# Attention units in tile order 0, 3, 1, 2; query products by pairs of tiles in two PSUM banks; the further 64 query latents held twice

## The chip, the cores and the metric

One core of one Trainium2 chip runs the whole kernel as one program. The metric is device time in microseconds (us); smaller is better. TensorE is called PE here, VectorE DVE, ScalarE ACT, GpSimd POOL and SyncE SP, as in the profile. A busy PE is not the same as a PE at its peak: a matmul's record has a drain behind the time for which it streams, and the next one starts beside that drain.

## The reference

Two layers on 4 sequences of 512 tokens with 256 features: latent attention with 16 heads, a mixture of 64 experts with 6 per token and a shared expert, a state-space layer, and a gated feed-forward layer with scales. All four are added to the residual. The change is in the attention, cut here to what matters:

```python
q = rmsnorm(x @ w_qa, q_norm_w) @ w_qb          # 192 latents -> 16 heads x (128 + 64)
q_nope, q_rope = q[..., :128], q[..., 128:]
kv = x @ w_kva                                  # 64 latents + 64 rotated key features
kv = rmsnorm(kv_c, kv_norm_w) @ w_kvb
q_rope, k_rope = rotate(q_rope), rotate(k_rope)
scores = einsum('blhd,bmhd->bhlm', q, k) / sqrt(192)
attn = softmax(where(causal_mask, scores, -1e30))
out = einsum('bhlm,bmhd->blhd', attn, v).reshape(B, L, 2048) @ w_o
```

## The kernel before, in words

The key and value weights are folded into the query and output weights beforehand (`prep_queries` L377, `prep_values` L392). So a head has 128 query features: 64 that meet the key's latents and 64 rotated ones. For each of the 4 sequences b, `project` (L452) makes the latents, and `latents` (L794) scales them into `cq1` (128 latents x 512 tokens) and `cq2` (the further 64 latents; rows 64 to 127 of `cq2` and `wqe2` are zeros that POOL writes at L979 and L980).

A **group** g is 4 heads of a sequence; a sequence has 4 groups, hg 0 to 3. A group has 16 **units**, u = 0 to 15: unit u is one head of one tile of 128 queries, tile i = u // 4, head u % 4. A causal tile i has (i+1) x 128 keys, so units are 128, 256, 384 and 512 wide, four of each, in this order. PE, ACT and DVE each walk the group in 16 **slots**, an order written out by hand:

- PE, `slot` L561: `scores` of unit `at` (L529, and a masking matmul in bf16, L530), a piece of the next group's query work, `transposes` of unit `at` - 3 (L538), then `values` (L555) at some slots. Each float32 matmul has two records in the trace.
- DVE, `slot` L886: `maximum` of unit `at` (L861), the reciprocal of the sum of unit `at` - 1 (L866), `evacuate` of unit `at` - 3 (L881, L884), `normalize` of unit `at` - 1 (L872), then perhaps a piece of the routing of the sequence before (`route_slot` L823; `weigh`, L1130, at slots 10, 12 and 14 of hg 2 and 3).
- ACT, `slot` L724: `exps` of unit `at` (L708), then copies of query products (`q_copy` L687, copy at L689), of their transposes (`qt_copy` L691, copy at L693) or of values (`take_values` L712, copy at L720).

Four PSUM banks hold scores, two transposes, one values (bank 6, `VALUE`), one the query products and their transposes (bank 7, `QUERY`). For the next group, `q_product` (L484) of tile i runs at slots 1, 3, 5, 7: `cq1` by 512 columns of weights (L488) and `cq2` by the same number (L489), both over 128 rows of the array. Each tile's product is copied by ACT, rotated by `rope` (L963: L972 to L976, POOL for these) and transposed (`q_transpose` L492, L494) at slots 9, 11, 13, 15. `values` runs three times per group, with tiles (0, 1), (2) and (3), at slots 12, 16 and 20; the last two fall into slots 0 and 4 of the group that follows. It writes two halves of the output's partitions (0 to 63 and 64 to 127), each from 64 columns of weights.

Between sequences PE runs `project`, `mean_squares` (L468, L469, L473), the `output` of the sequence (L617) and `first_queries` (L498): the four products of the next sequence's first group, in banks 7 and 6 in turn, and then their transposes. There POOL rotates tiles 0 and 2, DVE tiles 1 and 3 (`first_ropes` L808). In sequence b >= 1, PE also has in hg 0 the normalised tokens' transposes and the router's logits (`route_slot` L595, L1027), and in hg 1 the counts (L1035, L1036). POOL sends the tokens of the sequence before in hg 3's turns and after them (`att_pool` L978, sends at L1196).

What sets the order: every engine takes its instructions in program order, so a wait at one holds all behind it. A few of the waits:

```python
need(pe, A["exp"], NU * g + u - 3)              # scores(u): exp of unit u-4 done
pe.wait_ge(A["norm"], NU * g + u + 1)           # transposes(u)
pe.wait_ge(A["qs"], TB * (g + 1) + i)           # product i: copy of product i-1 done
pe.wait_ge(A["qte"], TB * (g + 1) + i)          # transpose i: copy of transpose i-1 done
act.wait_ge(A["max"], NU * g + u + 1)           # exp(u)
```

## Time and profile before

| | |
|---|---|
| median of 3 runs | 1339.31 us (1338.85 to 1340.66) |
| the profiled execution | 1338.7 us |
| its span | 1336.9 us |
| PE / DVE / ACT / POOL busy, share of the span | 92% / 61% / 34% / 28% |
| attention, from the first scores to the end of the last group | 58.8 us to about 620 us |
| mean granted TensorE clock | 0.967 of full speed |

The profiled execution's own time, 1338.7 us, is its span and 1.8 us around it. Rows below give the start of an instruction in us from the span's start and its duration. "<-" names what ended a wait.

### The profile page before, as it was taken

The page shows a single profiled execution, that of the slowest core. Times are in us where ns is not written, and L with a number is a line of the kernel's source. Part 1 is how long each engine was busy: PE and PEld are TensorE (multiplying, and loading weights), DVE is VectorE, ACT ScalarE, POOL GpSimd, SP SyncE. Part 2 cuts the span into 40 slices and gives each one's busy share as a digit, 9 for nine tenths or more (in the row PEclk, how much of TensorE's full clock was granted, in tenths as well). Part 3 has the DMA queues.
Part 4 walks back from the last instruction along what each step waited for, and adds up shares of the span by engine and source line. Part 5 has one row for each costly group of instructions (what it writes and reads, how often), then busy time and mean ns, then how long its engine had stood idle before and what let it go on. Part 6 is the DMA issues. An engine that isn't in the chain of part 4 may idle for free.

```text
span 1336.9 us, 19470 instructions
## 1 busy us (share of the span) xinstructions
PE 1231.2 (92%) x6004; PEld 760.4 (57%) x6004; DVE 813.2 (61%) x2238; ACT 454.2 (34%) x1041; POOL 378.8 (28%) x464
## 2 busy tenths in 40 slices
PE   6999999999999899998989999997578899899988
PEld 3566566555655556556556777775235446465454
DVE  6367767787578966785533333334576776676431
ACT  2455525453445425452201111110232533424311
POOL 1243013362425412362250000115364271510200
PEclk9799999999999999999999999998679899999999
DMA  9999999999900100011348888983111011100000
GB/s 317 413 420 420 420 421 419 420 419 417 420 35 28 68 1 1 1 52 44 101 129 256 259 266 273 285 260 118 48 55 48 24 52 36 37 12 17 0 16 16
DMA packets 89422, 235.48 MB, mean 176 GB/s; under 512 B 12769, under 2 KB 23681, under 8 KB 89089
## 3 DMA queue, kind: packets, MB, share of 16 engines
q1 hardware_dynamic: 70912, 192.54, 38.9%
q0 software_dynamic: 9216, 25.18, 5.9%
q10 hardware_dynamic: 9216, 16.78, 3.3%
q8 instruction: 42, 0.69, 0.2%
q14 instruction: 36, 0.29, 0.1%
HBM read 66.70 MB, written 167.77 MB: 175 GB/s over the span
## 4 chain that ended last, share of the span: by engine, by line
PE 69%; DVE 23%; issue 4%; POOL 2%; ACT 1%; DMA 1%; SPq 1%; ACTq 0%; POOLq 0%; DVEq 0%
PE bank L1329 5%; PE bank L529 5%; PE bank L617 4%; PE bank L488 4%; PE bank L1309 4%; PE bank L489 4%; PE bank L555 4%; DVE negmax L861 4%; PE bank L1582 3%; DVE r L872 3%; PE bank L1571 3%; PE bank L1565 3%; PE bank L538 3%; PE bank L1335 3%; PE bank L1294 2%
## 5 line engine op out<-in xcount | busy, mean ns | idle before, releaser
L708 ACT ACTIVATE r<-bank,negmax 128x128 f32<-128x128 f32 (+3 forms) x256 | 135.2, 528 | 174.3 <-DVE negmax L861 173.8
L529 PE MATMUL bank<-r 128*128 128x512 f32 (+3 forms) x512 | 184.3, 443 | 0.0
L861 DVE TENSOR_REDUCE negmax<-bank 128x1 f32<-128x128 f32 (+3 forms) x256 | 124.5, 487 | 44.6 <-PE bank L530 41.6
L972 POOL TENSOR_TENSOR r<-r,tables 128x256 f32<-128x256 f32 x56 | 42.0, 749 | 330.5 <-ACT r L689 330.3
L538 PE MATMUL bank<-tables,r 128*128 128x128 f32 x640 | 115.0, 278 | 12.2 <-DVE r L872 11.6
L1196 POOL DMA_INDIRECT sent<-r,slots x96 | 93.9, 978 | 99.8 <-DVE slots L1117 40.1
L1411 DVE COPY r<-bank 128x512 f32<-128x512 f32 x64 | 41.2, 686 | 120.5 <-PE bank L1335 76.2
L538 PEld LDWEIGHTS bank<-tables,r 128*128 128x128 f32 x640 | 72.7, 141 | 65.9 <-DVE r L872 31.4
L872 DVE TENSOR_SCALAR r<-r,rrow 128x128 f32<-128x128 f32 (+3 forms) x256 | 104.5, 408 | 0.3
L529 PEld LDWEIGHTS bank<-r 128*128 128x128 f32 x512 | 77.8, 191 | 23.6 <-issue 18.3
L1210 POOL DMA_INDIRECT r<-sent,slots x20 | 21.7, 1085 | 219.1 <-DVEq L1409 212.8
L1367 ACT ACTIVATE r<-bank 128x512 f32<-128x512 f32 x32 | 19.1, 597 | 184.8 <-PE bank L1309 184.8
L1525 POOL TENSOR_TENSOR r<-tables,r 128x1024 f32<-128x1024 f32 x16 | 33.8, 2113 | 142.2 <-DVE r L1946 119.6
L488 PE MATMUL bank<-r 128*128 128x512 f32 x128 | 70.0, 629 | 3.6 <-DVE x L816 1.6
L881 DVE COPY late<-bank 128x256 f32<-128x256 f32 (+1 forms) x128 | 60.7, 474 | 15.8 <-PE bank L538 15.7
L489 PE MATMUL bank<-r 128*128 128x512 f32 x128 | 66.3, 599 | 0.0
L1329 PE MATMUL bank<-r 128*128 128x256 f32 x256 | 63.8, 392 | 0.0
L1309 PE MATMUL bank<-r 128*128 128x256 f32 x256 | 61.7, 384 | 0.0
L617 PE MATMUL bank<-spent,r 128*128 128x256 f32 x256 | 57.9, 383 | 0.5 <-ACT r L720 0.5
L1571 PE MATMUL bank<-xnT,late 128*128 128x512 f32 (+1 forms) x96 | 48.6, 632 | 8.8 <-DVE spent L1599 8.8
L530 PE MATMUL bank<-futureb,identb 128*128 128x128 bf16 x256 | 56.1, 219 | 0.0
L1329 PEld LDWEIGHTS bank<-r 128*128 128x128 f32 x256 | 46.0, 189 | 17.2 <-issue 6.2
(266 smaller groups left out, 2390.5 us busy)
## 6 DMA issues: line engine op xcount, KB each, us to landing
sent<-gath SPq DMA_DIRECT2D x8, 16384.0 KB, 94.3
r<-waT_dram SPq DMA_DIRECT2D x64, 304.0 KB, 3.4
r<-sent SPq DMA_DIRECT2D x64, 256.0 KB, 3.4
sent<-r ACTq DMA_DIRECT2D x64, 256.0 KB, 4.1
w2buf<-wcT_dram SPq DMA_DIRECT2D x64, 48.0 KB, 3.5
r<-w_o_dram SPq DMA_DIRECT2D x1, 2048.0 KB, 11.0
sent<-gath SPq DMA_DIRECT2D x2, 1024.0 KB, 57.0
out_dram<-x SPq DMA_DIRECT2D x4, 512.0 KB, 2.9
```

The costliest lines, as they stand in the source:

```text
L488: nc.tensor.matmul(bank[at][:], cq1[:, i * P:(i + 1) * P], w1, start=True, stop=False)
L489: nc.tensor.matmul(bank[at][:], cq2[:, i * P:(i + 1) * P], w2, start=False, stop=True)\
L529: nc.tensor.matmul(at[:, 0:n], QT[g % 2][:, h, i * P:(i + 1) * P], KT[:, 0:n], start=True, stop=False)
L538: last = nc.tensor.transpose(bank[TRANS[u % 2]][:, j * P:(j + 1) * P], prob[:, u % 4, j * P:(j + 1) * P], ident)
L617: last = nc.tensor.matmul(bank[4 + i % 2][:, 0:DIM], OT[:, c, i * P:(i + 1) * P], wvo[:, c, :], start=(c == 0), stop=(c == HEADS // 2 - 1))
L708: nc.scalar.activation(prob[:, u % 4, 0:(i + 1) * P], bank[SCORE[u % 4]][:, 0:(i + 1) * P], ACT.Exp, bias=negmax[:, u:u + 1], scale=1.0, a ...
L861: nc.vector.tensor_reduce(negmax[:, u:u + 1], bank[SCORE[u % 4]][:, 0:(i + 1) * P], axis=AX.X, op=ALU.max, negate=True).then_inc(A["max"], 1)
L872: nc.vector.tensor_scalar(p, p, rrow[:, u:u + 1], None, ALU.mult).then_inc(A["norm"], 1)
L1196: nc.gpsimd.indirect_dma_start(sent[:, :], bass.IndirectOffsetOnAxis(ap=slots[:, t, k:k + 1], axis=0), xn1[:, n // TOPK, :], None).then_in ...
L1309: last = nc.tensor.matmul(bank[2][:, t * ROWS:(t + 1) * ROWS], wb[:, 2 * q + t, k * EI:k * EI + EA], tokens(q, t, k), start=(k == 0), stop ...
L1329: nc.tensor.matmul(to[t][:, half * DIM:(half + 1) * DIM], hid_a[:, q % 2, c:c + P], wb[:, 2 * q + t, KC * EI:KC * EI + DIM], start=(half = ...
L1571: last = nc.tensor.matmul(bank[up][0:w, :], fuT[:, k, lo:lo + w], xnT[:, k, row_tokens(f)], start=(k == 0), stop=(k == KC - 1))
```

## The change

- **Order of units.** `unit(u)` gives tile and head: units 0 to 7 alternate tile 0 and tile 3 over the 4 heads, units 8 to 15 tile 1 and tile 2. All of a tile's query work follows `ORDER` = (0, 3, 1, 2).
- **Values** run twice per group, tiles (0, 3) at slot 12 and (1, 2) at slot 20 (slot 4 of the next group).
- **Query products of two tiles at once.** `q_products(g, m)` makes tiles ORDER[2m] and ORDER[2m+1]. Bank 7 takes heads 0 and 1 of both, bank 6 heads 2 and 3 of both. Part 0: four matmuls of 256 columns with `cq1` over 128 rows. Part 1: four of 256 columns with `cq2` over 64 rows, rows 0 to 63 for bank 7 and 64 to 127 for bank 6. `cq2` holds the 64 latents twice, in both halves, and `wqe2` holds half of the heads in each half; the zeros and POOL's two memsets go. In a group hg 0 part 0 is at slots 1 and 3, otherwise at 6 and 8; part 1 is in the slot behind. ACT copies both banks in part 1's slot.
- **Turns** (transposes of the next group's queries): slots 9, 11, 13, 15 in hg 0; otherwise 11, 13, 14, 15.
- **Routing** of the sequence before is placed anew: the transposes at slots 6 and 8 and the logits at 10 (before 3, 6, 9); DVE's top and select one slot later; counts at slot 2 of hg 1 (before 7), and DVE's part behind them at slots 3 to 10 (before 8 to 15). `weigh` stays. POOL makes eight sends ahead of hg 3's turns rather than two behind each.
- **First queries of a sequence**: both pairs whole, one behind the other; the second waits for the copies of the first. POOL rotates the third tile once the second pair is copied.
- **Preparation**: the fourth bank goes, ACT makes 3 copies rather than 4, and DVE writes `cq2` twice (L800).

```diff
-        PRODUCT_AT = {1: 0, 3: 1, 5: 2, 7: 3}
-        TURN_AT = {9: 0, 11: 1, 13: 2, 15: 3}
-        VALUES_AT = {12: 0, 16: 1, 20: 2}
-        VALUE_TILES = ((0, 1), (2,), (3,))
+        Q_BANKS = (QUERY, VALUE)
+        PRODUCTS_AT = ({6: 0, 8: 1}, {1: 0, 3: 1})
+        TURN_AT = ({11: 0, 13: 1, 14: 2, 15: 3}, {9: 0, 11: 1, 13: 2, 15: 3})
+        VALUES_AT = {12: 0, 20: 1}
+        VALUE_TILES = ((0, 3), (1, 2))
+        ORDER = (0, 3, 1, 2)
+        def unit(u):
+            return VALUE_TILES[u // (2 * HG)][u % 2], u // 2 % HG
...
-            def q_product(g, i, at):
+            def q_products(g, m, parts=(0, 1)):
                 hg = g % GROUPS
...
+                two = 2 * QE
+                w2 = wqe2[:, 2 * hg:2 * hg + 2, :].rearrange("p h c -> p (h c)")
+                for t in range(2 if 0 in parts else 0):
+                    for half in range(2):
+                        w1 = wqe1[:, hg * HG + 2 * half:hg * HG + 2 * half + 2, :].rearrange("p h c -> p (h c)")
+                        nc.tensor.matmul(bank[Q_BANKS[half]][:, t * two:(t + 1) * two], cq1[:, q_tile(ORDER[2 * m + t])], w1,
+                                         start=(t == 0), stop=False)
+                for t in range(2 if 1 in parts else 0):
+                    for half in range(2):
+                        r = slice(QL2 * half, QL2 * (half + 1))
+                        last = nc.tensor.matmul(bank[Q_BANKS[half]][:, t * two:(t + 1) * two], cq2[r, q_tile(ORDER[2 * m + t])],
+                                                w2[r, :], start=False, stop=(t == 1))
+                        if t:
+                            last.then_inc(A["q"], 1)
...
             def first_queries(b):
...
+                pe.wait_ge(A["cq"], 3 * b + 3)
+                q_products(g, 0)
+                pe.wait_ge(A["qs"], TB * g + 2)
+                q_products(g, 1)
...
-                    if i == 0:
+                    if m == 0:
                         pe.wait_ge(A["qte"], TB * g + TB)
+                        need(pe, A["ote"], 2 * g)
...
                     else:
-                        pe.wait_ge(A["qs"], TB * (g + 1) + i)
-                    q_product(g + 1, i, QUERY)
+                        pe.wait_ge(A["qs"], TB * (g + 1) + 2)
+                    q_products(g + 1, m, (0,))
+                if not final and with_next and at - 1 in PRODUCTS_AT[first]:
+                    q_products(g + 1, PRODUCTS_AT[first][at - 1], (1,))
...
+            def q_copies(g, m):
+                two = 2 * QE
+                for half in range(2):
+                    act.wait_ge(A["q"], TB * g + 2 * m + half + 1)
+                    nc.scalar.copy(qs[:, 2 * m:2 * m + 2, half * two:(half + 1) * two],
+                                   bank[Q_BANKS[half]][:].rearrange("p (t c) -> p t c", t=2)).then_inc(A["qs"], 1)
...
+                    for half in range(2):
+                        nc.vector.scalar_tensor_tensor(out=cq2[QL2 * half:QL2 * (half + 1), :], in0=bank[1][0:QL2, :],
+                                                       scalar=qn2[:], in1=rq[0:QL2, :], op0=ALU.mult, op1=ALU.mult)\
+                            .then_inc(A["cq"], 1)
...
-                pool.wait_ge(A["qs"], TB * g + i + 1)
+                pool.wait_ge(A["qs"], TB * g + 2 * (i // 2) + 2)
```

## Rows read from the trace of the kernel before

**Rows 1.** The page's part on busy time: us, share, instructions.

```profile
PE 1231.2 (92%) x6004; PEld 760.4 (57%) x6004; DVE 813.2 (61%) x2238; ACT 454.2 (34%) x1041; POOL 378.8 (28%) x464
```

**Rows 2.** Windows, one group each: length, busy PE, PEld, DVE, ACT, POOL, clock, DMA.

```profile
82.83:111.02 28.19, 28.19 (x163) 17.22 (x160) 19.79 (x66) 15.54 (x44) 9.49 (x16) 1.00 1.02 420
...
226.18:257.01 30.83, 29.63 (x166) 17.96 (x164) 23.22 (x79) 15.40 (x46) 9.36 (x16) 1.00 1.02 420
257.01:287.54 30.53, 28.81 (x162) 17.21 (x160) 25.21 (x89) 15.51 (x46) 17.65 (x24) 1.00 1.02 419
287.54:308.16 20.62, 19.95 (x124) 11.77 (x121) 18.95 (x83) 10.08 (x34) 12.68 (x13) 1.00 1.02 418
139.23:158.99 19.76, 19.49 (x123) 11.73 (x121) 17.37 (x63) 10.88 (x35) 0.00 (x0) 1.00 1.03 420
```

**Rows 3.** Groups by line, 0 to 600 us, the query products.

```profile
L488 PE MATMUL bank<-r 128*128 128x512 f32 x128 | 70.0, 629 | 3.6 <-DVE x L816 1.6 <-issue 1.5
...
L489 PE MATMUL bank<-r 128*128 128x512 f32 x128 | 66.3, 599 | 0.0
```

**Rows 4.** Timeline of PE around `values` (L555) and `mean_squares` (L473).

```profile
75.89 0.50 PE L538 MATMUL bank<-tables,r 128*128 128x128 f32 x3
...
76.32 1.51 PE L555 MATMUL bank<-late,r 128*64 128x256 f32 x12
...
77.77 1.13 PE L529 MATMUL bank<-r 128*128 128x512 f32 x2
...
172.37 3.72 PE L617 MATMUL bank<-spent,r 128*128 128x256 f32 x16
...
176.02 1.12 PE L473 MATMUL bank<-r,ones 64*128 64x512 f32 x2
...
177.07 7.17 PE L617 MATMUL bank<-spent,r 128*128 128x256 f32 x32
```

**Rows 5.** Timeline of the weight loads of one 128-column unit.

```profile
88.07 0.30 PEld L529 LDWEIGHTS bank<-r 128*128 128x128 f32 x2
```

**Rows 6.** Timeline of one 512-wide unit on its way from scores to normalised.

```profile
80.42 0.22 PE L530 MATMUL bank<-futureb,identb 128*128 128x128 bf16 x1
...
80.67 0.69 DVE L861 TENSOR_REDUCE negmax<-bank 128x1 f32<-128x512 f32 x1
...
81.35 0.54 DVE L881 COPY late<-bank 128x384 f32<-128x384 f32 x1
81.40 0.69 ACT L708 ACTIVATE r<-bank,negmax 128x512 f32<-128x512 f32 x1 [0.43 <-DVE negmax L861]
...
81.81 0.48 DVE L872 TENSOR_SCALAR r<-r,rrow 128x512 f32<-128x512 f32 x1
...
82.20 0.68 DVE L861 TENSOR_REDUCE negmax<-bank 128x1 f32<-128x512 f32 x1
...
82.92 0.69 ACT L708 ACTIVATE r<-bank,negmax 128x512 f32<-128x512 f32 x1 [0.74 <-DVE negmax L861]
...
83.60 0.58 ACT L693 COPY r<-bank 128x512 f32<-128x512 f32 x1
```

**Rows 7.** Timeline of the first queries of sequence 1.

```profile
188.80 1.12 PE L488 MATMUL bank<-r 128*128 128x512 f32 x2 [0.52 <-DVE x L816]
...
194.92 0.72 POOL L972 TENSOR_TENSOR r<-r,tables 128x256 f32<-128x256 f32 x1 [1.08 <-ACT r L689]
...
195.97 0.59 ACT L689 COPY r<-bank 128x512 f32<-128x512 f32 x1 [1.13 <-PE bank L489]
...
196.55 0.72 POOL L976 TENSOR_TENSOR r<-r 128x256 f32<-128x256 f32 x1
...
198.97 0.39 PE L529 MATMUL bank<-r 128*128 128x128 f32 x2
```

**Rows 8.** Timeline of DVE around one `weigh` in hg 3 of sequence 1.

```profile
302.60 0.27 DVE L1133 SCALAR_TENSOR_TENSOR scratch<-r,scratch 128x64 f32<-128x64 f32 x1
...
303.54 0.56 DVE L861 TENSOR_REDUCE negmax<-bank 128x1 f32<-128x384 f32 x1
```

More of the change, by code:

```diff
@@ L385, in prep_queries @@
                                  start=True, stop=True)
-                last = nc.tensor.matmul(bank[6 + h // 8][0:QL2, c:c + KVL], wqbT[:, h, P:QL], wkvT[:, 0, h, :],
+                r, c = QL2 * (h // 2 % 2), (h // 4 * 2 + h % 2) * KVL
+                last = nc.tensor.matmul(bank[6][r:r + QL2, c:c + KVL], wqbT[:, h, P:QL], wkvT[:, 0, h, :],
                                         start=True, stop=True)
@@ L394, in prep_values @@
             loaded(pe, "w_o")
[L395 removed]
+            pe.wait_ge(prep_out, 3)
             pe.wait_ge(A["kr"], 1)
@@ L406, in prep_queries_out @@
             act.wait_ge(prep_w, 1)
-            for m in range(2):
-                for dst, b, n in ((wqe1, 4, P), (wqe2[0:QL2], 6, QL2)):
-                    nc.scalar.copy(dst[:, 8 * m:8 * m + 8, 0:KVL],
-                                   bank[b + m][0:n, :].rearrange("p (h c) -> p h c", h=8)).then_inc(prep_out, 1)
+            for dst, at in ((wqe1[:, 0:8], 4), (wqe1[:, 8:16], 5), (wqe2, 6)):
+                nc.scalar.copy(dst[:, :, 0:KVL], bank[at][:].rearrange("p (h c) -> p h c", h=8)).then_inc(prep_out, 1)
         def prep_values_out(act):
@@ L522, in scores @@
             def scores(g, u):
-                i, h = u // HG, u % HG
+                i, h = unit(u)
                 n = (i + 1) * P
@@ L533, in transposes @@
             def transposes(g, u):
-                i = u // HG
+                i, _ = unit(u)
                 pe.wait_ge(A["norm"], NU * g + u + 1)
@@ L543, in values @@
                 tiles = VALUE_TILES[n]
[L544 to L545 removed]
+                pe.wait_ge(A["pte"], NU * g + 2 * HG * (n + 1))
+                need(pe, A["ote"], 2 * g + n)
                 if n == 0 and g % GROUPS == 0:
                     need(pe, R["lgs"], g // GROUPS)
[L548 to L551 removed]
+                for m, i in enumerate(tiles):
+                    c = 2 * P * m
                     for j in range(i + 1):
@@ L704, in exps @@
             def exps(g, u):
-                i = u // HG
+                i, _ = unit(u)
                 act.wait_ge(A["max"], NU * g + u + 1)
@@ L717, in take_values @@
                 hg = g % GROUPS
-                for i in tiles:
-                    c = 2 * P * (i - tiles[0])
+                for m, i in enumerate(tiles):
+                    c = 2 * P * m
                     last = nc.scalar.copy(OT[:, 2 * hg:2 * hg + 2, i * P:(i + 1) * P],
@@ L858, in maximum @@
             def maximum(g, u):
-                i = u // HG
+                i, _ = unit(u)
                 dve.wait_ge(A["s"], NU * g + u + 1)
@@ L868, in normalize @@
             def normalize(g, u):
-                i = u // HG
+                i, _ = unit(u)
                 p = prob[:, u % 4, 0:(i + 1) * P]
@@ L993, in att_pool @@
                 for hg in range(1, GROUPS):
+                    if b and hg == GROUPS - 1:
+                        send_ready(pool, b - 1)
+                        for n_sent in range(2 * TB):
+                            send(b - 1, n_sent)
                     for i in range(TB):
                         turn(GROUPS * b + hg, i)
-                        if b and hg == GROUPS - 1:
-                            if i == 0:
-                                send_ready(pool, b - 1)
-                            send(b - 1, 2 * i)
-                            send(b - 1, 2 * i + 1)
                 if b:
```

143 lines of the change are left out of this document (62 added, 81 removed).

## The prediction

> **What bounds the kernel now.** I read the busy times first: PE is busy for 92% of the span, DVE for 61% [rows 1]. An average over stages says little, so the windows of single groups came next [rows 2]. Of sequence 0's group 1 (28.19 us) PE is busy for all of it, DVE for 19.79 us, 1.24 us per slot. The last group of sequence 0, which has no query work for a next one, takes 19.76 us: DVE needs 17.37, so the two run close. In sequences 1 to 3 groups hg 1 and 2 take 30.83 and 30.53 us; the reader should see that PE's busy share falls there and DVE's rises. So attention is bound by PE where products are made, with DVE near behind elsewhere.
>
> **What PE saves.** A record of 512 columns streams for 0.43 us: two matmuls are four such records, and the groups by line give 0.55 and 0.52 us of union per record [rows 3], drains and half clock included, while the timeline gives 0.86 us for the two records of L473 less the joints below. So a product of one tile costs 1.72 us, of which L489 0.86.
>
> The price of changing the array's shape can be read off a timeline [rows 4]. L538's three records start at 75.89 and stream 0.32; `values` starts at 76.32, 0.11 late. Its 12 records of 256 columns (0.216 us each alone) take 1.45 us until the next start, where six steps of two at once make 1.30; L529 then loses 0.11 more (1.13 against 1.02). Together about 0.45 us per `values`, and the halves do run at once. For 64 rows of the array: L617's 16 records stream 3.46 from 172.37, and L473 starts 0.19 behind that; it takes 1.05 for 0.86. Counting the slow first record behind the joint, I take 0.40 us per stretch of 64 rows.
>
> - *Part 1.* Two tiles' L489 cost 1.72. After: four matmuls of 256 columns, eight records; two at once make four steps, 0.86, plus 0.40. Saved 0.45 per pair, in 24 pairs inside groups: 10.8. No row shows two halves of the array's rows at work at once, only halves of the columns [rows 4]. Bounds: fully together (saves 0.45) and one after the other (costs 0.40). Each half needs a 128-column weight load per record; loads are 0.11 us apart [rows 5], so two fit a step of 0.216. I take fully together, by the nearest row, `values`.
> - The Trainium skill ("TensorE: Matmul & The Clock Gate", Part 3, on packing small matmuls) states 3.07 times for four row tiles, not 4; by that share two tiles would give about 1.5 times, an estimate, part 1 would cost 1.15 + 0.40, the pair would save 0.17 rather than 0.45, and the whole would come out at 1355. The trace shows no such loss for column halves [rows 4], and the sum stays with them.
> - *Values* lose one joint of three per group: 16 x 0.45 = 7.2. The same ten steps of work stay.
> - *Half as many starts of a product behind the bf16 matmul*: 24 x 0.06 = 1.4, an estimate from the 0.05 us by which such a first record runs over.
> - *Preparation*: one ACT copy of 0.5 us less before the first product: 0.5. The second `cq2` write on DVE (0.73 us, as the first) lies beside PE's prep matmuls in sequence 0 and beside L617 in the others; without that cover it would cost 4 x 0.73. The two memsets of POOL are off the path. POOL's eight sends ahead of hg 3's turns take about 8 x 1.27 = 10 us and begin some 4 us before hg 2 does; the first copy there comes about 14 us in, so they are hidden.
>
> Sum of savings: 19.9 us.
>
> **What it adds in waits.** PE's queue is in order, and the pieces now sit so that the next one is due before its copy is made. The chain of a unit [rows 6]: masking matmul at 80.42, maximum at 80.67, exp at 81.40; exp to the next ACT work 0.68 (82.92 to 83.60). So ACT is free 0.25 + 0.73 + 0.68 = 1.66 us after the masking matmul's start of a 512-wide unit, 1.42 of a 384-wide one (maximum and exp some 0.12 shorter each).
>
> 1. *Second pair, slot 8 (hg 1, 2).* From slot 7's masking matmul: part 1 ends at 1.29; ACT, behind its exp, copies two banks from 1.66 to 2.81 (0.55 and 0.59). PE does part 1, one transpose and a 256-wide score, and is ready at 1.92. Wait 0.94, 8 groups: 7.5. In hg 0 part 1 stands beside a 128-wide unit: copies end at 2.5, PE is ready at 2.24: 4 x 0.3 = 1.2.
> 2. *Turn at slot 14.* The one at 13 and this one share bank 7. The copy of the former stands behind exp 13: 1.42 + 0.58 + 0.05 = 2.05; PE is ready after 0.06 + 0.44 + 0.22 + 0.49 = 1.21. Wait 0.84, 8 groups: 6.7. The turn at 15 has a full slot between and waits for nothing.
> 3. *Slots 0 to 4.* Before, light units of DVE and PE came together. Now each two slots hold a long and a short unit: DVE needs some 1.2 us in every slot, but PE only 3.4 in slots 0 to 3 together. DVE's slot: maximum to evacuation to normalise to next maximum 80.67, 81.35, 81.81, 82.20 [rows 6], 1.53 with a 512-wide maximum and normalise; with the other kinds of neighbours 1.06 to 1.22. Following both queues from slot 15, unit 1 is normalised 5.1 us in, while PE stands at its transpose at 4.4: a wait of 0.8 counting the step from one engine to the next. 12 groups: 9.6. Against it: the counts fill it in 3 groups (-2.4), before had such waits of 0.5 in four groups hg 3 and six groups of sequences 1 to 3 (-5.0); `weigh` at slot 14, 0.94 us [rows 8], makes it longer in 3 groups (+2.9). Net 5.1.
> 4. *Slots 5 to 12 without products.* In hg 3 PE's work from slot 5 to the transposes of unit 9 is 6.0 us, DVE's chain is 8.2 (1.08 to 1.40 a slot, and 1.65 us from a 512-wide maximum to its reciprocal): wait 2.25, against some 0.85 before: 4 x 1.4 = 5.6. In hg 0 turns fill some: 1.35 in sequence 0; in the others the router's parts fill it but wait for ACT's copies at slots 7 and 9 and for the logits' copy at 12: 1.5 each. Together 11.4.
> 5. *First queries of sequences 1 to 3* [rows 7]. Before, four products in two banks ran without a wait, the last copy ended at 196.56 (7.76 after 188.80), scores came at 198.97 (10.17). After: a pair takes 3.0; copies to 4.3; the second pair to 7.3; copies to 8.6. Only then does POOL rotate the third tile: 2.35 us (194.92 to 197.27), so until 11.05, and two transposes of 0.45 follow. Scores come at 12.1. 3 x 1.9 = 5.7. In sequence 0 the value preparation (L401, 3.7 us) stands between and covers it.
>
> Sum of added waits: 8.7 + 6.7 + 5.1 + 11.4 + 5.7 = 37.6 us.
>
> **What it takes away in waits.** Sequences 1 to 3 before: hg 1 took 30.83 where sequence 0's took 28.19 [rows 2], of the 2.64 the counts are 0.87 and slot 0's wait 0.5 (counted above); hg 2 was 2.34 longer, 0.5 of it at slot 0. The rest, 3 x (1.3 + 1.8) = 9.3, are turns that wait while DVE routes ahead of a maximum. The routing of hg 1 now lies at slots 3 to 10, beside PE's long slots. I take 8.2 as given back; the bounds are 0 and 9.3.
>
> The sum: -19.9 + 37.6 - 8.2 = +9.5 us on the profiled execution's 1338.7, so 1348.2. The median of the runs is 0.6 above that execution, within their spread; I say 1348. The expert loop and all behind attention stay as they are.
>
> The Trainium skill has a rule that speaks against the change ("TensorEngine Tiling (Array Packing)", PSUM Bottleneck): when tiling makes TensorE faster, the copies out of PSUM may become the limit. The trace bears this out in a way of its own [rows 6], since a copy stands behind the exp; the sum would be the same without it.
>
> **Rivals.**
> - *Faster, the waits of DVE don't form.* Items 3 and 4 rest on my walk through two queues. For it: PE waits at slots 8 and 14 give DVE slack, DVE is busy 19.79 of 28.19 [rows 2], and POOL and ACT are idle half the time. Against: DVE's lead isn't stored, it can't run before the scores are there. Without items 3 and 4 the sum is 9.5 - 16.5 = -7.0: 1332. If the slot 8 and 14 waits are also half as long, -14: 1325. It decides at the point where DVE's slot costs less than PE's over slots 0 to 3, some 0.85 us.
> - *Row halves one after the other.* Part 1 then costs 1.72 + 0.40 rather than 1.26: 24 x 0.86 = 20.6 and 5 in first queries: 1374. For it: no row shows them together; against it: `values` shows halves of columns together, and loads at 0.11.
> - *The routing's waits stay* (nothing given back): 1356.
>
> **How the numbers follow.** Forecast (waits outweigh the saving): 0.54, of it 0.08 within 0.2%; DVE's waits small: 0.34, of it 0.05 within 0.2%; halves in turn: 0.12. 0.2%, about 2.7 us, is what a measurement of this kernel can tell from no change. So faster 0.30, same 0.13, slower 0.57. The range reaches down to 1326, which leaves the fastest outcomes of the first rival out, and up to 1364, which leaves out the halves in turn. The forecast's own range is 1341 to 1358.
>
> **What would show it.** Right: group 1 of sequence 0 at about 29.3 us rather than 28.19; PE waits of nearly 1 us for ACT's product copies at slot 8 and for the copy of a turn at slot 14; L538 waiting for DVE's L872 in slots 4 to 10; part 1's eight records in about 0.86 us; first queries of a sequence 12 us long. Wrong: sequence 0's group 1 under 28 us; or part 1's records at 0.216 us intervals one by one; or, if hg 1 and 2 of sequences 1 to 3 stay over 30.5, the relief.

## The result

The changed kernel takes 1381.41 us (median of 4 runs, 1378.28 to 1388.24), the kernel before 1339.92 beside it on the same chip. The ratio is 1.0317, with a 95% interval of 1.0278 to 1.0357: slower, and outside the range of 1326 to 1364. The direction was right, the size was not. The profiled executions have spans of 1379.8 and 1336.9 us, so the traces differ by 42.9 us. The profiled execution of the changed kernel took 1382.0 us, inside the spread of its four runs.

The profile's page after (busy times, the clock's slices, three of the groups by line):

```profile
PE 1222.5 (89%) x6260; PEld 786.3 (57%) x6260; DVE 828.0 (60%) x2242; ACT 445.2 (32%) x1040; POOL 380.8 (28%) x462
...
PEclk9899999999999999999999999999589999999999
...
L554 PE MATMUL bank<-tables,r 128*128 128x128 f32 x640 | 117.8, 282 | 25.7 <-DVE r L896 25.1
...
L501 PE MATMUL bank<-r 128*128 128x256 f32 x256 | 65.0, 398 | 20.3 <-ACT r L710 13.6
...
L513 PE MATMUL bank<-tables,r 128*128 128x128 f32 x256 | 38.1, 276 | 21.0 <-ACT r L715 10.2
```

PE's share is down from 92% [rows 1] to 89%. L554, the transposes of the softmax weights (L538 before), is the same 640 records, but PE stands 25.7 us in front of them. Before it was this, from the page of the kernel before:

```profile
L538 PE MATMUL bank<-tables,r 128*128 128x128 f32 x640 | 115.0, 278 | 12.2 <-DVE r L872 11.6
```

In front of the part 0 products (L501) and of the turns (L513) it now stands 20 and 21 us, mostly for ACT's copies L710 and L715.

The windows of single groups after, which answer to [rows 2] (hg 1 of sequence 0; hg 3 of sequence 0; hg 0, 1 and 2 of sequence 1):

```profile
84.17:114.02 29.85, 27.58 (x178) 18.60 (x176) 20.21 (x67) 14.55 (x44) 9.63 (x16) 1.00 1.02 420
...
143.72:165.11 21.39, 19.53 (x126) 11.96 (x124) 17.74 (x61) 10.83 (x35) 0.00 (x0) 1.00 1.02 418
...
207.49:237.30 29.81, 27.18 (x174) 19.43 (x172) 19.20 (x67) 15.92 (x44) 9.21 (x16) 1.00 1.02 420
237.30:271.26 33.96, 29.02 (x183) 19.34 (x181) 26.39 (x89) 15.06 (x45) 12.93 (x19) 1.00 1.02 420
271.26:302.74 31.48, 27.73 (x179) 18.59 (x176) 23.82 (x87) 14.46 (x44) 15.01 (x22) 1.00 1.02 420
```

The first two rows are near what was forecast: 29.85 us (29.3 forecast, 28.19 before) and 21.39 (21.2 by item 4 alone, 19.76 before). The other three aren't. Hg 1 of sequence 1 takes 33.96 us where it took 30.83, and hg 0 29.81 where before it took this:

```profile
199.19:226.18 26.99, 26.53 (x146) 16.76 (x144) 18.64 (x71) 15.70 (x42) 9.40 (x16) 1.00 1.02 420
```

Adding the groups by kind, from the masking matmul of one group's first unit to that of the next, and the forecast's terms in the same way (all in us):

| stretch | before | after | measured | forecast |
|---|---|---|---|---|
| 4 groups hg 0 | 104.2 | 114.8 | +10.6 | +1.2 |
| 4 groups hg 1 | 121.1 | 131.7 | +10.6 | hg 1 and 2 |
| 4 groups hg 2 | 119.1 | 124.0 | +4.9 | together -4.7 |
| 4 groups hg 3, to their last unit | 81.6 | 88.4 | +6.8 | +7.9 |
| 3 passages between sequences | 125.7 | 131.3 | +5.6 | +5.7 |
| ahead of the first unit, behind the last | 785.1 | 789.5 | +4.4 | -0.5 |
| sum | 1336.8 | 1379.7 | +42.9 | +9.6 |

(The forecast's terms are rounded one by one here; its sum was 9.5.) One thing shifts between these rows, and the column of the forecast leaves it out. With tiles (0, 3) first and 384- and 256-wide units last, a group does more of its own values and transposes before it ends and hands less to what follows. Counting PE's records in the two traces by their columns (0.43 us for 512), the new order moves 5.2 us of work into the four groups hg 0 and 0.9 into hg 3, out of the passages (4.5) and the last stretch (1.5); no work is added by it. Against a forecast with this shift in it, hg 0 is 4.2 us over, hg 1 and 2 together 20.2, the passages 4.4 and the last stretch 6.4, while hg 3 is 2.0 under. So the passages only seem to come out as forecast: of the 33 us that are missing, most lies in hg 1 and 2 of sequences 1 to 3, which route the sequence before, and some 11 in the passages and behind attention.

**How the pieces look in the trace.** Part 1 with 64 rows of the array, in slot 9 of that first group:

```profile
101.84 0.22 PE L546 MATMUL bank<-futureb,identb 128*128 128x128 bf16 x1
...
101.99 1.14 PE L506 MATMUL bank<-r 64*128 64x256 f32 x8
...
103.06 0.33 PE L554 MATMUL bank<-tables,r 128*128 128x128 f32 x1
```

Eight records of 256 columns (0.216 us each alone) take 1.07 us until the next start (L554 at 103.06). One by one they begin in pairs 0.007 us apart, at 101.992 and 101.999, then at 102.312, 102.528 and 102.744: the two halves of the array's rows work at once. The first pair starts 0.15 behind the masking matmul and holds 0.32 instead of 0.216; part 1 costs about 1.2 us in all, and 1.26 was forecast. The rival "row halves one after the other" falls here, and so does the theory below that they cost more than they save.

The turn at slot 14 of the same group:

```profile
110.35 0.58 ACT L730 ACTIVATE r<-bank,negmax 128x384 f32<-128x384 f32 x1 [0.84 <-DVE negmax L885]
...
110.92 0.58 ACT L715 COPY r<-bank 128x512 f32<-128x512 f32 x1
...
111.64 0.63 PE L513 MATMUL bank<-tables,r 128*128 128x128 f32 x4 [0.77 <-ACT r L715]
```

The turn waits for the copy of the former, which stands behind an exp. From masking matmul to masking matmul the slot takes 2.43 us, of which its work makes 1.47: a wait of 0.96, forecast 0.84. At slot 8 it is 1.02 by the same reckoning, forecast 0.94. (The profile's idle time, 0.77 and 0.82 us, is shorter, because a record's drain covers the start of a wait.)

The routing in sequence 1's hg 1, slots 6 to 8, is where the forecast fails:

```profile
248.30 0.41 DVE L1117 TENSOR_TENSOR r<-scratch,bank 128x256 f32<-128x256 f32 x1
...
248.86 1.97 PE L501 MATMUL bank<-r 128*128 128x256 f32 x8 [1.33 <-DVE r L1117]
...
252.62 0.43 DVE L1123 TENSOR_TENSOR r<-r,scratch 128x256 f32<-128x256 f32 x1
...
253.08 0.69 DVE L885 TENSOR_REDUCE negmax<-bank 128x1 f32<-128x512 f32 x1
...
254.48 1.06 ACT L710 COPY r<-bank 128x512 f32<-128x512 f32 x2
...
255.60 1.99 PE L501 MATMUL bank<-r 128*128 128x256 f32 x8 [1.61 <-ACT r L710]
```

Two waits, both on DVE's account. The pair of slot 6 overwrites a bank that DVE's ranks (L1117) still read, so it stands 1.33 us. Then DVE routes (L1123 at the last) ahead of the maximum of slot 7; maximum, exp and the two copies behind it all slide, and the pair of slot 8 stands 1.61 us. Slots 6 and 8 take 4.64 and 4.74 us here, 3.14 and 3.95 in sequence 0.

In hg 0 of sequence 1 the same happens with the router's copies, which ACT makes behind its exps. PE waits 1.23 us at slot 8 (below) and 0.83 at slot 10:

```profile
221.35 0.69 ACT L730 ACTIVATE r<-bank,negmax 128x512 f32<-128x512 f32 x1 [1.44 <-DVE negmax L885]
222.03 0.57 ACT L361 COPY xnT<-bank 128x512 f32<-128x512 f32 x1
222.66 0.66 PE L355 MATMUL bank<-tables,r 128*128 128x128 f32 x4 [1.23 <-ACT xnT L361]
```

### The profile page after: what moved, and what is told of

The parts are those of the page before. It is cut to its first block, busy times and chain, and to the rows that moved or that the text cites. A ratio compares the mean times of both kernels' runs of the same rounds, so it can differ in the third digit from the quotient of the medians.

```text
span 1379.8 us, 19972 instructions
## 1 busy us (share of the span) xinstructions
PE 1222.5 (89%) x6260; PEld 786.3 (57%) x6260; DVE 828.0 (60%) x2242; ACT 445.2 (32%) x1040; POOL 380.8 (28%) x462
## 4 chain that ended last, share of the span: by engine, by line
PE 62%; DVE 24%; issue 5%; ACT 4%; POOL 2%; DMA 1%; SPq 1%; ACTq 0%; POOLq 0%; DVEq 0%
PE bank L501 5%; PE bank L569 5%; PE bank L1351 4%; PE bank L1331 4%; DVE negmax L885 4%; PE bank L1604 3%; PE bank L1593 3%; PE bank L545 3%; DVE r L896 3%; PE bank L1587 3%; PE bank L636 3%; PE bank L1357 2%; PE bank L1316 2%; PE bank L1338 2%; PE bank L554 2%
## 5 line engine op out<-in xcount | busy, mean ns | idle before, releaser
L545 PE MATMUL bank<-r 128*128 128x256 f32 (+3 forms) x512 | 183.6, 441 | 0.0
L554 PE MATMUL bank<-tables,r 128*128 128x128 f32 x640 | 117.8, 282 | 25.7 <-DVE r L896 25.1
L554 PEld LDWEIGHTS bank<-tables,r 128*128 128x128 f32 x640 | 72.5, 142 | 72.8 <-DVE r L896 49.6
L896 DVE TENSOR_SCALAR r<-r,rrow 128x128 f32<-128x128 f32 (+3 forms) x256 | 101.2, 395 | 0.3
L501 PE MATMUL bank<-r 128*128 128x256 f32 x256 | 65.0, 398 | 20.3 <-ACT r L710 13.6
L501 PEld LDWEIGHTS bank<-r 128*128 128x128 f32 x256 | 47.1, 194 | 35.5 <-ACT r L710 20.2
L905 DVE COPY w2buf<-bank 128x512 f32<-128x512 f32 x64 | 43.6, 681 | 37.2 <-PE bank L554 37.2
L1351 PE MATMUL bank<-r 128*128 128x256 f32 x256 | 63.8, 392 | 0.0
L1331 PE MATMUL bank<-r 128*128 128x256 f32 x256 | 62.4, 388 | 0.0
L513 PE MATMUL bank<-tables,r 128*128 128x128 f32 x256 | 38.1, 276 | 21.0 <-ACT r L715 10.2
```

Source lines behind the costliest of these rows:

```text
L501: nc.tensor.matmul(bank[Q_BANKS[half]][:, t * two:(t + 1) * two], cq1[:, q_tile(ORDER[2 * m + t])], w1, start=(t == 0), stop=False)
L545: nc.tensor.matmul(at[:, 0:n], QT[g % 2][:, h, i * P:(i + 1) * P], KT[:, 0:n], start=True, stop=False)
L554: last = nc.tensor.transpose(bank[TRANS[u % 2]][:, j * P:(j + 1) * P], prob[:, u % 4, j * P:(j + 1) * P], ident)
L896: nc.vector.tensor_scalar(p, p, rrow[:, u:u + 1], None, ALU.mult).then_inc(A["norm"], 1)
L905: nc.vector.tensor_copy(prob_at(i)[:, :, h, :], src.rearrange("p (j l) -> p j l", j=i + 1))\
L1331: last = nc.tensor.matmul(bank[2][:, t * ROWS:(t + 1) * ROWS], wb[:, 2 * q + t, k * EI:k * EI + EA], tokens(q, t, k), start=(k == 0), stop ...
```

## The experiments

Three theories. **Placement**: the concurrency works as priced, and the loss is a number of separate waits of pieces put where their copy isn't made yet; each can be mended alone, the gains add up. **Order**: the new order of units sets DVE's pace in most groups, and undoing it brings most back. **Shape**: row halves and joints cost more than they save; the records of part 1 above settle this one.

The changed kernel's interval, 1.0278 to 1.0357, overlaps with that of every version of it below but two (the unsplit products with the turns moved back, and all together). For the others the difference in time alone shows nothing, and the readings are from the traces: lengths of groups, and the waits in them. Sums of groups are taken as in the table above.

### The order undone in the new kernel

```diff
-        VALUE_TILES = ((0, 3), (1, 2))
-        ORDER = (0, 3, 1, 2)
+        VALUE_TILES = ((0, 1), (2, 3))
+        ORDER = (0, 1, 2, 3)
...
-            return VALUE_TILES[u // (2 * HG)][u % 2], u // 2 % HG
+            return u // HG, u % HG
```

> The changed kernel with units and tiles in the old order 0, 1, 2, 3 and values in two calls, (0, 1) and (2, 3); the paired products, their slots and the routing stay as changed. Placement theory (most of the 41 us are PE's waits at slots 6, 8, 10 and 14, for ACT's copies and DVE's routing, and stay here; the alternation costs some 15 to 20): 1360 to 1367, with waits of about 1 us still at slots 8 and 14 of group 1. Order theory (the alternation, by DVE being needed 1.2 us in every slot, costs most of it): 1345 or less.

Measured: 1385.93 us, 1.0327 [1.0304, 1.0351] of before. The time doesn't come back, and both forecasts missed (1360 to 1367, and 1345 or less). Hg 0 is 4.3 us shorter than in the changed kernel, hg 3 4.3, hg 1 2.4, hg 2 0.6; the passages take 142.9 rather than 131.3. Of that, 4.5 us are the work that the old order leaves for them, and 5.2 us of work go out of hg 0; some 5 are the clock, which falls to half at the end of every sequence (stretches of 3.4, 6.8 and 3.4 us in the passages, where the changed kernel has one of 3.4). The waits of 1 us expected at slots 8 and 14 of sequence 0's hg 1 are idle times of 0.09 and 0.48 here. PE waits 22.9 us for DVE to normalise, in attention as a whole, and 22.5 in the changed kernel: the old order with two values calls takes none of it away.

### Two values calls in the old kernel

```diff
-        VALUES_AT = {12: 0, 16: 1, 20: 2}
-        VALUE_TILES = ((0, 1), (2,), (3,))
+        VALUES_AT = {12: 0, 20: 1}
+        VALUE_TILES = ((0, 1), (2, 3))
...
```

> The kernel before with values of tiles 2 and 3 in one call at slot 20, so one joint of the array's shape less per group; nothing else. If a joint costs 0.45 us and PE is the bound: 16 x 0.45 = 7.2 less, 1333. If the longer stretch at slot 4 only moves waits, 1338 to 1341.

Measured: 1364.21 us, 1.0158 [1.0133, 1.0182]. One joint less per group was to save 7 us, and moved waits were to make 1338 to 1341; the kernel loses 22 (26.7 in the profiled execution). Hg 1, 2 and 3 are 3.8, 2.8 and 4.6 us longer, the passages 8.2, and what lies ahead of and behind attention 7.3, the most of it clock. In hg 1 and 2 slot 0 has no values any more, and PE's first product stands behind ACT's copy of the last turn (waits of PE in attention, 60 to 633 us: us in total, times, longest):

```profile
PE bank L538 <- DVE r L872: 18.7, 29, 2.0
PE bank L488 <- ACT r L693: 8.1, 8, 1.3
```

The second of these doesn't exist before, the first is 9.1 there. The end of sequence 0 shows how the first comes about. Timeline of PE before, then with two calls:

```profile
159.93 0.66 PE L538 MATMUL bank<-tables,r 128*128 128x128 f32 x4 [0.28 <-DVE r L872]
160.52 1.52 PE L555 MATMUL bank<-late,r 128*64 128x256 f32 x12
161.97 1.33 PE L538 MATMUL bank<-tables,r 128*128 128x128 f32 x8
```

```profile
163.47 0.66 PE L538 MATMUL bank<-tables,r 128*128 128x128 f32 x4 [0.27 <-DVE r L872]
165.12 0.66 PE L538 MATMUL bank<-tables,r 128*128 128x128 f32 x4 [1.00 <-DVE r L872]
166.18 0.66 PE L538 MATMUL bank<-tables,r 128*128 128x128 f32 x4 [0.40 <-DVE r L872]
```

Before, 1.5 us of values (L555) lie between two sets of transposes, and the next eight records run through. Taken out, PE only waits for DVE to normalise instead: 1.00 and 0.40 us. Then the clock falls. Windows of that end and of the project behind it, with two calls:

```profile
162.54:166.67 4.13, 2.47 (x19) 1.76 (x17) 4.13 (x11) 1.55 (x4) 0.00 (x0) 1.00 1.02 421
166.67:174.90 8.23, 8.23 (x26) 3.58 (x26) 1.92 (x4) 1.78 (x3) 0.00 (x0) 0.79 1.02 422
```

PE is busy 2.47 of 4.13 us, and the granted clock of the next 8.23 us is 0.79, because 3.4 us of it stand at half (1.2 of 2.4 GHz). The other three sequences have such a stretch at their end as well (6.8 us at the last), and the stretches at half clock make 110.1 us of the execution where they made 89.7.

### The new order alone in the old kernel

```diff
-        VALUES_AT = {12: 0, 16: 1, 20: 2}
-        VALUE_TILES = ((0, 1), (2,), (3,))
+        VALUES_AT = {12: 0, 20: 1}
+        VALUE_TILES = ((0, 3), (1, 2))
+        ORDER = (0, 3, 1, 2)
+
+        def unit(u):
+            return VALUE_TILES[u // (2 * HG)][u % 2], u // 2 % HG
...
```

> The kernel before with only the order of units (tiles 0 and 3, then 1 and 2) and the two calls of values; products of one tile at slots 1, 3, 5, 7, turns and routing where they were. Placement theory: the PE-light slots 1 and 3 are filled by products in hg 0, 1 and 2, so only hg 3 loses (about 1.6 us each), two calls save 7: 1335 to 1345. Order theory: 1365 or more.

Measured: 1351.96 us, 1.0067 [1.0044, 1.0091]. It lies between the two forecasts. Order and two values calls together cost about 9 us, 6 to 12 by the interval. Hg 1 and 2 are within 0.8 of before (+0.6, -0.8). Hg 0 is 2.9 longer, but PE waits 0.2 us there in all: it is work that before fell behind the group. Hg 3 is 7.3 longer, 0.9 of it such work, and PE waits 9.7 us for DVE to normalise there (1.9 before): where PE has no product to make, DVE's pace shows. That is item 4 of the forecast. The last stretch is 4.4 longer, with 10.1 us more at half clock, which make 5. All this is a quarter of the loss; the order theory, which asked for 1365 or more, falls.

Beside the run before, this says more. Two values calls cost 22 us with the old order and 10 with the new one, so the two belong together. What the order costs by itself, with three calls, no run shows.

### The second pair of first queries in other banks

```diff
-                pe.wait_ge(A["qs"], TB * g + 2)
-                q_products(g, 1)
+                if b:
+                    q_products(g, 1, banks=TRANS)
+                else:
+                    pe.wait_ge(A["qs"], TB * g + 2)
+                    q_products(g, 1)
...
```

> The changed kernel, in sequences 1 to 3 with the second pair of first queries in the two transposes' banks, so that it waits for no copy. If the wait for the copies (1.16 us at 199.46) holds the whole chain behind it: 3 x 1.2 = 3.5 less, 1378. If the last rotation on POOL were bound by something else than the second pair's copies: no difference, 1381.

Measured: 1380.61 us, 1.028 [1.0253, 1.0307] of its own before; against the changed kernel no difference shows, as the second forecast had it, though not for its reason. In the changed kernel the second pair waits for the copies of the first (first fence); in banks 4 and 5 it starts 1.2 us sooner (second fence):

```profile
195.24 1.99 PE L501 MATMUL bank<-r 128*128 128x256 f32 x8 [0.52 <-DVE x L840]
...
199.46 1.99 PE L501 MATMUL bank<-r 128*128 128x256 f32 x8 [1.16 <-ACT r L710]
```

```profile
198.23 1.99 PE L501 MATMUL bank<-r 128*128 128x256 f32 x8
...
202.54 1.06 PE L513 MATMUL bank<-tables,r 128*128 128x128 f32 x8 [1.25 <-ACT r L713]
205.12 1.97 PE L513 MATMUL bank<-tables,r 128*128 128x128 f32 x8 [1.51 <-POOL r L1004]
```

Only one of three passages keeps the gain (output's end to the next scores 11.92 instead of 13.14 us). In the other two the clock falls at 205 and 369 us, right behind waits of 1.25 and 1.51 us for the copies and POOL's rotation, and the last eight turns take 1.97 us for 1.06.

### ACT copies the turn ahead of its exp

```diff
+                first = g % GROUPS == 0
+                if at < NU and with_next and at in TURN_AT[first]:
+                    qt_copy(g + 1, TURN_AT[first][at], QUERY)
                 if at < NU:
                     exps(g, at)
...
-                if at < NU and with_next and at in TURN_AT[first]:
-                    qt_copy(g + 1, TURN_AT[first][at], QUERY)
```

> The changed kernel with ACT's copy of a turn ahead of the exp of its slot. Theory (PE's wait at slot 14 of hg 1 and 2 is for a copy that stands behind an exp): that slot falls from 2.43 us (3.53 in hg 2 of later sequences) to about 1.6, so 8 x 0.85 + 3 x 0.7 = 9 less, 1372. Rival (the exp, now later by 0.4, holds DVE and PE's transposes instead): 1380 or more.

Measured: 1378.69 us, 1.0269 [1.0231, 1.0308], between the two forecasts. The wait itself goes, but for 0.25 us:

```profile
109.83 0.59 ACT L715 COPY r<-bank 128x512 f32<-128x512 f32 x1 [0.68 <-PE bank L513]
110.31 0.59 ACT L730 ACTIVATE r<-bank,negmax 128x384 f32<-128x384 f32 x1
110.56 0.63 PE L513 MATMUL bank<-tables,r 128*128 128x128 f32 x4
```

The copy is now ahead of the exp and the next turn starts at once; slot 14 takes 1.72 us everywhere (2.43 before, 3.53 in sequence 1's hg 2). Hg 1 and 2 gain 2.8 and 3.6 us, hg 0 1.0; together 7.4. The passages give 2.6 back, hg 3 and the last stretch 1.2 more, and the stretches at half clock grow from 102.2 to 109.0 us, which make 3.4: each sequence's end now has the clock fall.

### Part 1 not split off, and then the turns where they were

```diff
-                    q_products(g + 1, m, (0,))
-                if not final and with_next and at - 1 in PRODUCTS_AT[first]:
+                    q_products(g + 1, m, (0,) if first else (0, 1))
+                if first and not final and with_next and at - 1 in PRODUCTS_AT[first]:
...
-                if at < NU and with_next and at - 1 in PRODUCTS_AT[first]:
-                    q_copies(g + 1, PRODUCTS_AT[first][at - 1])
+                if at < NU and with_next and at - first in PRODUCTS_AT[first]:
+                    q_copies(g + 1, PRODUCTS_AT[first][at - first])
```

> The changed kernel with both parts of a pair in one slot (6 and 8) in hg 1 and 2, and ACT's two copies in that slot, behind a short unit's exp. Theory (slot 8's wait comes from the split: the copies stand behind the exp of a 512-wide unit): the wait of 1.0 at slot 8 goes in 8 groups, and the 0.8 more of it in hg 1 of sequences 1 to 3 in part: 10 less, 1371. Rival (ACT and DVE starve behind the longer stretch and the wait moves to slots 9 and 10): 1380.

The second kernel has this line as well:

```diff
-        TURN_AT = ({11: 0, 13: 1, 14: 2, 15: 3}, {9: 0, 11: 1, 13: 2, 15: 3})
+        TURN_AT = ({9: 0, 11: 1, 13: 2, 15: 3}, {9: 0, 11: 1, 13: 2, 15: 3})
```

> The same, and the turns at slots 9, 11, 13, 15 in all groups. Theory (placement alone makes the loss against the kernel with only the order changed, 1352): slot 14's waits go too, 11 more, so 1360. Rival (two pairs through two banks cost as much wherever they stand): 1372 or more.

Measured: 1380.10 us (1.0293 [1.0257, 1.0328]) and 1369.09 (1.021 [1.0175, 1.0245]). The first is the rival's figure, the second lies between theory and rival. Unsplit, slots 6 to 9 of sequence 0's hg 1 take 9.71 us instead of 10.71, so the wait of slot 8 is gone, and the group takes 29.10 us for 29.85. In sequence 1's hg 1 the 1.61 us of slot 8 are gone as well, but waits of 0.71 and 1.26 us for DVE to normalise stand at slots 10 and 12 instead, and the group takes 34.28 for 33.96. With the turns back at 9, 11, 13, 15 sequence 0's group is at last shorter than before:

```profile
84.44:112.53 28.09, 27.41 (x179) 18.45 (x177) 20.11 (x66) 14.73 (x44) 9.80 (x16) 1.00 1.02 419
```

28.09 us against 28.19 [rows 2], and all four groups hg 2 together take 117.8 against 119.1. PE is busy 27.41 us there rather than 28.19. So two tiles at once, with one values call less (the run doesn't part them), do save PE's time, where the pieces stand well.

### The routing of hg 1 later

```diff
                 if hg == 1 and at == 3:
                     route.running(c, QUERY, (0, 1))
-                if hg == 1 and at == 4:
                     route.running(c, QUERY, (2, 3))
-                if hg == 1 and at == 5:
+                if hg == 1 and at == 4:
                     route.ranks(c, QUERY)
-                if hg == 1 and at == 6:
+                if hg == 1 and at == 5:
                     route.upper(c)
                 if hg == 1 and at == 7:
                     route.downward(c)
-                if hg == 1 and at == 8:
-                    route.nearest(c)
                 if hg == 1 and at == 9:
+                    route.nearest(c)
+                if hg == 1 and at == 11:
                     route.places(c)
...
-                if hg == 1 and at == 10:
+                if hg == 1 and at == 12:
                     route.shares(c)
```

> The changed kernel with DVE's routing of hg 1 packed otherwise: running at slot 3, ranks 4, upper 5, downward 7, nearest 9, places 11, shares 12. Theory (PE waits 1.33 us at slot 6 for the ranks, and at slot 8 0.8 more than in sequence 0, since DVE routes ahead of a maximum): 3 x 2.1 = 6 less, 1375. Rival (DVE has no slack there and the same work shows elsewhere): 1381.

Measured: 1376.17 us, 1.0255 [1.0219, 1.0292], as the theory had it. The four groups hg 1 take 124.4 us instead of 131.7; in sequence 1 slot 6 is back at 3.14 us and slot 8 at 3.95, just as in sequence 0. The two causes read off the timeline above are the whole of it at these slots. They were taken away together, so their shares rest on the timeline. The passages take 1.7 us more.

### The turn's copy ahead of the exp, in the old kernel

```diff
+                if at < NU and with_next and at in TURN_AT:
+                    qt_copy(g + 1, TURN_AT[at], QUERY)
                 if at < NU:
                     exps(g, at)
...
-                if at < NU and with_next and at in TURN_AT:
-                    qt_copy(g + 1, TURN_AT[at], QUERY)
```

> The kernel before with ACT's copy of a turn ahead of the exp of its slot; nothing of the change. Theory (before, turns at slots 11 and 15 of hg 1 and 2 in sequences 1 to 3 wait for a copy behind an exp that DVE's routing delays, about 0.7 to 1.0 and 0.4 to 0.9 us per group): 6 groups x 1.0 = 6 less, 1334. Rival (the exp is later, and a transpose or the end of the sequence waits in its place, as the end of the sequences did with the changed kernel's copies moved): 1338 to 1342.

Measured: 1339.43 us, 0.9999 [0.9979, 1.0019]. Waits do go (slot 11 of sequence 1's hg 1 takes 1.69 us for 2.48), but slot 0 of that group and of the next grows (2.81 to 3.32 us, 2.93 to 3.80): there PE meets DVE's pace instead, and its waits for DVE to normalise grow from 9.1 to 15.9 us. Hg 0 and 1 are 1.0 and 1.6 us shorter, hg 3 is 2.6 longer. What helps the changed kernel isn't to be had in the old one.

### ACT makes the router's copies ahead of its exps

```diff
+                first = g % GROUPS == 0
+                if g >= GROUPS and first and at in (7, 9):
+                    norm_evacuate(act, nc.scalar.copy, N1, g // GROUPS - 1, at // 9)
                 if at < NU:
                     exps(g, at)
...
-                    if at == 7:
-                        norm_evacuate(act, nc.scalar.copy, N1, g // GROUPS - 1, 0)
-                    if at == 9:
-                        norm_evacuate(act, nc.scalar.copy, N1, g // GROUPS - 1, 1)
```

> The changed kernel with the evacuations of the router's two transposes ahead of ACT's exps of slots 7 and 9 in hg 0 of sequences 1 to 3. Theory (hg 0's loss of 2.8 us per group there is PE's wait for these evacuations at slots 8 and 10, each behind an exp): 3 x 1.5 = 4.5 less, 1377. Rival (the waits at 8 and 10 are DVE's, for the normalised units, as in hg 3): 1381.

Measured: 1374.92 us, 1.0254 [1.0217, 1.0291], somewhat more than the theory's 1377. Sequence 1's hg 0 takes 27.25 us instead of 29.81: slot 8 falls from 3.22 to 1.77, slot 10 from 4.03 to 2.94. All of hg 0 is 107.2 (114.8 in the changed kernel, 104.2 before); hg 2 and the passages are 2.1 and 2.8 longer.

### All five together

```diff
+        TURN_AT = ({9: 0, 11: 1, 13: 2, 15: 3}, {9: 0, 11: 1, 13: 2, 15: 3})
...
+                if b:
+                    q_products(g, 1, banks=TRANS)
...
+                    q_products(g + 1, m, (0,) if first else (0, 1))
...
+                if g >= GROUPS and first and at in (7, 9):
+                    norm_evacuate(act, nc.scalar.copy, N1, g // GROUPS - 1, at // 9)
+                if at < NU and with_next and at in TURN_AT[first]:
+                    qt_copy(g + 1, TURN_AT[first][at], QUERY)
+                if at < NU:
+                    exps(g, at)
+                if at < NU and with_next and at - first in PRODUCTS_AT[first]:
+                    q_copies(g + 1, PRODUCTS_AT[first][at - first])
```

and the routing of hg 1 as above (added lines alone are shown).

> The changed kernel with all the mended places together: both parts in one slot and turns at 9, 11, 13, 15; turn copies ahead of exps; routing of hg 1 packed; the second pair of first queries in other banks; the evacuations of the router's transposes ahead of the exps of slots 7 and 9. Theory (the loss is the sum of separate waits, each of which goes with its cause; what stays is the order's 9 and first queries): 1369 - 7 for hg 1 - 4 for hg 0 - 2 = 1356. Rival (each wait taken away is taken up by the next engine's): 1365 or more.

Measured: 1357.73 us, 1.0133 [1.0095, 1.0171] of before. That is 23.7 us under the changed kernel and near the theory's 1356; the rival's 1365 falls. The placement theory holds for over half of the loss. Hg 1 and 2 are now shorter than before (120.3 and 116.0 us against 121.1 and 119.1). What stays is in hg 3 (92.0 against 81.6), in hg 0 (+2.4), in the passages (+3.2) and behind attention (+4.8). The chief of PE's waits in this kernel's attention, 60 to 622 us (engine and line, what it waits for: us in total, times, longest):

```profile
PE bank L557 <- DVE r L896: 30.4, 59, 1.5
PE bank L513 <- ACT r L713: 6.4, 6, 1.2
PE bank L513 <- POOL r L1001: 4.5, 3, 1.5
```

The same view before, 60 to 611 us:

```profile
PE bank L538 <- DVE r L872: 9.1, 22, 0.9
```

With the copies out of the way, 30.4 us of waiting for DVE to normalise are left where there were 9.1. What they belong to is not shown. Order and two values calls in the old kernel have 17.1 of it, two calls with the old order 18.7, so the two calls are at least as likely a cause as the order; the changed kernel with three values calls was not run. No version beat the kernel before.

## Why the prediction was wrong

The mechanism it named, waits of misplaced pieces that outweigh what PE saves, is what happened; it was mis-sized, 9.5 us where 42.9 came. The step that failed most is "What it takes away in waits", -8.2 us: nothing was given back, and new waits came in its place. The other steps that failed are the clock and the ends of the sequences, put at nothing, and item 4 in hg 0.

Right:
- *The price of part 1*: 1.26 us forecast, about 1.2 measured, the row halves at once. By the estimate there from the Trainium skill ("TensorE: Matmul & The Clock Gate", Part 3), part 1 would cost 1.55; the trace shows no such loss for two halves (four steps hold eight records, the first 0.32 us, the others 0.216).
- *Items 1 and 2 in sequence 0*: 0.94 and 0.84 forecast, 1.02 and 0.96 measured (the 0.3 of item 1 in hg 0 did not come). *Item 3*: about 0.8 forecast at slot 4, 0.7 measured. *Item 4 in hg 3*: +7.9 for hg 3 with item 3's share, +6.8 measured, 0.9 of it work and not waits.
- *Item 5*: scores were to come 12.1 us behind the first product, they come at 207.27, 12.03 behind 195.24. That the passages as a whole came out at +5.6 is luck: less work, more waits and a fall of the clock cancelled.
- The Trainium skill's rule from "TensorEngine Tiling (Array Packing)", PSUM Bottleneck, that copies out of PSUM can become the limit, fits, in the way the prediction named: PE waits for copies that stand in ACT's queue behind an exp, while ACT as a whole is busy 32% of the span.

Wrong:
- *"What it takes away in waits", -8.2 us.* The bounds of that step were 0 and 9.3 given back. Before, the six groups hg 1 and 2 of sequences 1 to 3 were together 14.7 us longer than if each had been as long as sequence 0's; after, 17.6. With item 3's terms for the same groups (counts and slot 0) the forecast had 13.6 less, and 2.9 more came: 16.5 of the 33 us. I had counted only that DVE's routing would have slack beside long slots. Overlooked was, first, that the product pair shares a bank with the ranks (wait of 1.33 us), and second, that DVE's routing stands ahead of the maximum, behind which exp and product copies queue. The bound "not below 0" had no row behind it. Moving the routing by one or two slots takes both waits away (slots 6 and 8 back at sequence 0's length, 7.3 us in the four groups). The rival "the routing's waits stay", at 1356, points the right way and is still too small. In hg 2 only 0.5 us a group came back where 1.8 were counted.
- *Item 4 in hg 0 of sequences 1 to 3, 1.5 us each.* PE stands idle 1.23, 0.83 and 0.53 us at slots 8, 10 and 12 of sequence 1's hg 0. The group is 2.82 us longer as a whole, 1.3 of it work moved in by the order. The first two waits are for ACT's router copies behind exps: the run with these ahead gives 2.56 back.
- *Item 2 in hg 2 of sequence 1*: 2.06 us at slot 14, not 0.84; the weighing of the routing (DVE, four of L1155 in a row, the last below) stands ahead of the maximum there, and exp and copy stand behind that:

```profile
298.15 0.28 DVE L1155 SCALAR_TENSOR_TENSOR scratch<-r,scratch 128x64 f32<-128x64 f32 x1
...
298.47 0.56 DVE L885 TENSOR_REDUCE negmax<-bank 128x1 f32<-128x384 f32 x1
...
299.64 0.58 ACT L715 COPY r<-bank 128x512 f32<-128x512 f32 x1
...
300.36 0.63 PE L513 MATMUL bank<-tables,r 128*128 128x128 f32 x4 [1.88 <-ACT r L715]
```

- *Savings of 19.9 us.* In sequence 0's hg 1 PE's busy time is 0.6 us less (28.19 to 27.58), and part 1's records stream 1.7 us less than L489's did, before the joints; by the lengths of the slots without their waits the work is some 1.3 less, as against 1.5 forecast. But the 7.2 us of the values' joints can't be shown to reach the path. In the old kernel, the values call that goes is what covered DVE (1364.21 us): the joint's price was read rightly and the cover that came with it put at nothing.
- *"Without that cover it would cost 4 x 0.73".* The second `cq2` write delays the key latents behind it: PE waits 0.49 us for DVE's L828 there in each later sequence, costed at nothing.

```profile
190.62 0.46 PE L489 MATMUL bank<-tables,r 64*128 64x64 f32 x4 [0.49 <-DVE r L828]
```

- *"The expert loop and all behind attention stay."* From the last unit on, the execution takes 730.8 us instead of 726.1, and the clock isn't in the prediction at all. The stretches at half clock grow from 89.7 to 102.2 us; 9.1 of that are behind the last unit, 6.8 of them at the end of attention, and 9.1 us at half clock make 4.6. The other runs go the same way: where no fall follows the last unit, that stretch takes 726.0 (the old kernel with the turn's copy ahead); where 3.4 us follow, 727.2 to 728.0; where 6.8 or more, 730.2 to 731.7. At the end of sequence 2, PE stands 1.59 and 0.59 us for DVE, and the project behind it takes 7.01 us for its 12 records. Sequence 1 ends with almost the same waits, 1.52 and 0.59, and there the clock stays, so these waits alone don't decide it:

```profile
489.56 0.44 PE L554 MATMUL bank<-tables,r 128*128 128x128 f32 x2 [1.59 <-DVE r L896]
490.59 0.55 PE L554 MATMUL bank<-tables,r 128*128 128x128 f32 x3 [0.59 <-DVE r L896]
490.98 7.01 PE L469 MATMUL bank<-xnT,w_a 128*128 128x512 f32 x12
```

Before, in the same place (L460): 

```profile
466.17 5.32 PE L460 MATMUL bank<-xnT,w_a 128*128 128x512 f32 x12
```

Open: how much of hg 3's loss, and of the 30.4 us of waiting for DVE, a third values call would save (values at slot 16 kept with tile pairs); what the order costs without the two calls; and what makes the clock fall at one end of a sequence and not at another. None was tried.

## What to carry to other kernels

A saving on the bounding engine is only worth what the in-order queues beside it let through: before moving a piece, list for every slot who reads the bank it writes, and what stands ahead of its copy in the copying engine's queue, in the stage where that engine is busiest, not in the plainest one. A piece of PE work between two things that wait for another engine is cover; removing it may give nothing, and the granted clock may fall behind the new waits, as it did here. And a relief that is "given back" needs a lower bound below zero, unless a row excludes a new wait.

## What the runs showed of the hardware

- Two fp32 matmuls on 64 rows each, in different halves of the array's rows, run at once at full rate: pairs of records 0.007 us apart, pairs 0.216 apart, with a first pair of 0.32. The trace before showed this only for halves of the columns.
- A wait can cost more than itself. Behind the stretch with two values calls where PE was busy 2.47 of 4.13 us, the granted clock stood at half (1.2 GHz) for 3.4 us, and 12 records took 7.01 us rather than 5.32. With ACT's turn copies moved ahead, such a fall came at the end of every sequence, and about half of the 7.4 us gained in hg 0 to 2 was given back.
